# One expert's projection gathered into a block of twelve matmuls, and the first silu moved to the chunk before, in a time-mix and mixture-of-experts kernel

## The chip, the cores and the metric

The kernel runs on one core of one Trainium2 chip. The metric is the device time of one execution in microseconds (us); lower is better.

## The reference

The input is 4 batches of 1024 tokens with 128 features. Two time-mix layers (layer norm, three 128x128 projections k, v, r, a decaying scan over time, an output projection) are added to the input and layer-normed. A router then picks for each token the two best of 8 experts, each expert takes at most 307 tokens of a batch, and every expert computes this on its rows:

```
x = _layernorm(x + time_mix(x))
logits = x @ router_w + router_b            # top 2 of E = 8, softmax of the two
h = einp2 @ w_c_fc + b_c_fc                 # 128 -> 512
g = einp2 @ w_gate + b_gate                 # 128 -> 512
o = silu(h * g) @ w_c_proj + b_c_proj       # 512 -> 128
x = _layernorm(x + sum over the two experts of prob * o)
```

## The kernel before, in words

All work is written out by hand, engine by engine, in one order for each engine; semaphores tie them. After a head (batches 0 and 1 are mixed, batch 0 is routed) the program is four periods, one for each batch b. A period has 32 points: point = 4 e + j, for expert e (0 to 7) and chunk j (0 to 3) of the expert's 512 hidden features.

At each point TensorE first runs `hidden_pair` (L778 to L780): three matmuls for the gate and three for the up projection, with 308 columns, into one of two pairs of PSUM banks (pair0 at even points, pair1 at odd). ScalarE copies the gate out with its bias (`gate_copy`, L984), VectorE multiplies (`product`, L1299, prod_made). The pair of banks is free again when that product is made, so `hidden_pair` of a point waits for the product two points earlier:

```
                if c >= 2 or later(b):
                    pe.wait_ge(prod_made, nth(b, POINTS, c - 1))
```

ScalarE applies silu to two chunks at a time (`silu`, L991): chunks 0 and 1 of expert e at its point j = 2, chunks 2 and 3 at point j = 0 of the next expert. TensorE multiplies the result by the projection weights (`project`, L795, output ps_o) one expert behind, in twelve pieces (four chunks by three blocks of 104 rows; each piece shows as two records). VectorE copies ps_o out (`copy_out`, L1311), at j = 0 of the expert after the next. The last expert of a batch is projected whole at point 1 of the next period.

Between these, tables name what else each engine does at a point, before its next point. On TensorE: transposes for the mixing (`turn`, L619), the k, v, r matmuls (`kvr`, L639 to L651), `out` (L679), router logits (L695), counts (L709 to L724), transposes of expert rows (`turn_slots`, L756, at points 6, 18, 28, 29, 30). On ScalarE copies of the same (L912, L929, L939, L968). On VectorE `slots_low` (L1161), the mixing (`kv_of`, `scan_of`: L1112, L1122, L1127), statistics and norms (L1070, L1076, L1095), the combine of a finished batch (first_sum L1252, second_sum L1261, final_norm L1287). The mixing of batch b + 2 stands in period b, so only periods 0 and 1 have it; period 2 has the routing of batch 3, and period 3 has only the last combines. After period 3 comes a tail that adds the last batch's experts.

Of the kernel before, what the change touches and what calls it, by code (L numbers as in the profile page):

```python
# [37 lines left out]
B, T, L = 4, 1024, 2  # L38
# [5 lines left out]
E, K, H = 8, 2, 512  # L44
HC = H // P
# [3 lines left out]
PARTS = 3  # L49
# [110 lines left out]
               15: [("scales", 3)], 16: [("spread", 0)], 21: [("spread", 1)], 22: [("spread", 2)],  # L160
               23: [("spread", 3)], 24: [("spread", 4)], 29: [("spread", 5)]}

PIECES = ({j: tuple(range(4 * (j - 1), 4 * j)) for j in (1, 2, 3)}, {2: tuple(range(6)), 3: tuple(range(6, 12))})
PIECES_LAST = {1: tuple(range(6)), 2: tuple(range(6, 12))}
SLOT_TURNS = {6: (0, 3), 18: (0, 4), 28: (1, 0), 29: (1, 1), 30: (1, 2)}


# [7 lines left out]
def nth(b, per, k):  # L175

    return b * per + k


def step(b, n):  # L180


    return nth(b, 4, n + 1) if n < 4 else nth(b, 2, n - 3)
# [17 lines left out]
def later(b):  # L201

    return b > 0


def time_mix_moe(nc, h, ln_w, ln_b, Wk, Wv, Wr, Wo, router_w, router_b, w_fc, b_fc, w_gate, b_gate,
                 w_proj, b_proj, out):
    with ExitStack() as ctx:
# [379 lines left out]
        def _(pe):  # L588
# [142 lines left out]
            def turn_slots(b, g):  # L731
                mixed = min(step(b + 1, 3), 4 * B)
                if g == 0:
                    pe.wait_ge(r_copied, mixed)
                    pe.wait_ge(turned_sb[1], step(b, 5))
                if g == 1:
                    pe.wait_ge(k_copied, mixed)
                    pe.wait_ge(x_added, mixed - 1)
                    pe.wait_ge(rows_made, b + 1)
                if g == 2:  # L740
                    pe.wait_ge(kv_made, mixed)
                    pe.wait_ge(x_added, mixed)
                    pe.wait_ge(logits_copied, nth(b, 2, 2))
                if g < 2 and later(b):
                    pe.wait_ge(slots_copied, nth(b - 1, GROUPS, 4 + g))
                if g >= 3:
                    pe.wait_ge(slots_copied, nth(b, GROUPS, g - 2))
                if g == 3 and b + 1 < B:
                    pe.wait_ge(turned_sb[1], step(b + 1, 5))
                if g == 4 and b + 1 < B:  # L750
                    pe.wait_ge(rows_made, b + 2)
                if g == 4 and b + 2 < B:
                    pe.wait_ge(x_added, step(b + 2, 0))
                pe.wait_ge(slots_loaded[g], nth(b, 16, 16))
                for j in range(4):
                    mm = nc.tensor.transpose(bank[g % 3][:, P * j:P * j + P], slot_x[:, g % SLOT_RING, j, :],  # L756
                                             ident[:, :])
                mm.then_inc(slots_turned, 1)

            def hidden_pair(b, e, j):  # L760

                c = e * HC + j
                cols = slice(e * SLOTS, e * SLOTS + COLS)
                chunk = slice(P * j, P * j + P)
                if j == 0:
                    pe.wait_ge(slots_copied, nth(b, GROUPS, (e * SLOTS + COLS - 1) // (4 * P) + 1))
                if c == 0 and not later(b):
                    for read in (r_copied, k_copied, kv_made):
                        pe.wait_ge(read, nth(1, 4, 4))
                    pe.wait_ge(rows_made, 1)  # L770
                    pe.wait_ge(pool_low_made, 2 * LOW_BY_POOL)
                    pe.wait_ge(vector_low_made, 2 * (E - LOW_BY_POOL))
                    pe.wait_ge(x_added, step(1, 3))
                if c >= 2 or later(b):
                    pe.wait_ge(prod_made, nth(b, POINTS, c - 1))
                for which, (hi, lo, made) in enumerate(((gate_hi, gate_lo, g_made), (fc_hi, fc_lo, h_made))):
                    ps = pair[c % 2][which][:, 0:COLS]
                    nc.tensor.matmul(ps, hi[:, e, chunk], slotT_hi[:, cols], start=True, stop=False)  # L778
                    nc.tensor.matmul(ps, hi[:, e, chunk], slotT_lo[:, cols], start=False, stop=False)  # L779
                    nc.tensor.matmul(ps, lo[:, e, chunk], slotT_hi[:, cols], start=False, stop=True).then_inc(made, 1)  # L780

            def project(b, e, pieces):

                for piece in pieces:
                    c, part = divmod(piece, PARTS)
                    if piece == 0:
                        pe.wait_ge(hidden_made, nth(b, 2 * E, 2 * e + 1))
                        if e or later(b):
                            pe.wait_ge(o_copied, nth(b, E, e))
                        else:  # L790
                            pe.wait_ge(proj_in, 16 * E)
                            pe.wait_ge(x_added, step(1, 3))
                    if piece == 2 * PARTS:
                        pe.wait_ge(hidden_made, nth(b, 2 * E, 2 * e + 2))
                    mm = nc.tensor.matmul(ps_o[0:PART, P * part:P * part + P],  # L795
                                          hidden[:, e % 2, c, PART * part:PART * part + PART], proj_sb[:, e, c, :],
                                          start=(piece == 0), stop=(c == HC - 1), skip_group_check=True)
                    if piece == HC * PARTS - 1:
                        mm.then_inc(o_made, 1)
# [54 lines left out]
            def period(b):  # L854
                for point in range(POINTS):
                    e, j = divmod(point, HC)
                    hidden_pair(b, e, j)
                    if b == LAST:
                        for name, n in TENSOR_LAST.get(point, ()):
                            last_stages[name](n)  # L860
                    if b + 1 < B:
                        for name, n in TENSOR_ROUTE.get(point, ()):
                            stages[name](b + 1, n)
                    if e > 0:
                        project(b, e - 1, (PIECES[b + 2 < B] if nth(b, E, e) + 1 < B * E else PIECES_LAST).get(j, ()))
                    if point == 1 and b > 0:
                        project(b - 1, E - 1, range(HC * PARTS))
                    if point in SLOT_TURNS:
                        ahead, g = SLOT_TURNS[point]
                        if b + ahead < B:  # L870
                            turn_slots(b + ahead, g)
                    if b + 2 < B:
                        for name, n in TENSOR_MIX.get(point, ()):
                            stages[name](b + 2, n)
# [9 lines left out]
            for b in range(B):  # L884
                period(b)
# [10 lines left out]
        def _(act):  # L896
# [80 lines left out]
            def gate_copy(b, e, j):  # L977
                c = e * HC + j
                act.wait_ge(g_made, nth(b, POINTS, c + 1))
                if c == 0 and not later(b):  # L980
                    act.wait_ge(small_in, 16 * 2)
                if c >= 2 or later(b):
                    act.wait_ge(prod_made, nth(b, POINTS, c - 1))
                nc.scalar.activation(gate_s[:, c % 2, :], pair[c % 2][0][:, 0:COLS], ACT.Identity,  # L984
                                     bias=bgate_sb[:, e, j:j + 1]).then_inc(g_copied, 1)
# [19 lines left out]
            def period(b):  # L1005
                for point in range(POINTS):
                    e, j = divmod(point, HC)
                    gate_copy(b, e, j)
                    if b == LAST:
                        for name, n in SCALAR_LAST.get(point, ()):  # L1010
                            last_stages[name](n)
                    if j == 0 and e > 0:
                        silu(b, e - 1, 1)
                    if point == 0 and b > 0:
                        silu(b - 1, E - 1, 1)
                    if j == 2:
                        silu(b, e, 0)
                    if b + 1 < B:
                        for name, n in SCALAR_ROUTE.get(point, ()):
                            stages[name](b + 1, n)  # L1020
                    if point in SLOT_TURNS:
                        ahead, g = SLOT_TURNS[point]
                        if b + ahead < B:
                            copy_slots(b + ahead, g)
                    if b + 2 < B:
                        for name, n in SCALAR_MIX.get(point, ()):
                            stages[name](b + 2, n)
# [16 lines left out]
            for b in range(B):  # L1044
                period(b)
# [616 lines left out]
```

## Time and profile before

| what | value |
|---|---|
| median of 3 runs | 366.13 us (363.21 to 367.05) |
| profiled execution, first to last instruction | 382.6 us |
| TensorE busy in it | 332.7 us (87%) |
| VectorE, GpSimd, ScalarE busy | 262.8, 203.9, 166.2 us |
| periods 0, 1, 2, 3 in it | 69.94, 71.53, 68.19, 64.19 us |

The profile is of one execution, with its own time, longer than the median of the timed runs; the times give no other number for it. Its matmul ends are modelled. A matmul's record is longer than the time until the next one starts, so work on TensorE is best read from start to start. The same holds for VectorE, where records overlap by some 0.09 us.

### The profile page before, as it was taken

Reading aid. Unit: us, or ns where it says so; the run is one execution under the profiler, and the core shown is the slowest. Engines: PE = TensorE matmul, PEld = TensorE weight load, DVE = VectorE, ACT = ScalarE, POOL = GpSimd, SP = SyncE. Lnnn points to the kernel's source line nnn. Section 1 sums busy time; section 2 is a strip of 40 time slices with the busy share of each in tenths; the row PEclk is TensorE's granted clock in tenths of the full one; section 3 lists DMA queues with packets and bytes.
Section 4 is the critical chain, followed back from the end, with each engine's and each line's share of the span. In section 5 each row is a group of like instructions: output and inputs, shape, how many; then the busy total and the mean of one; then the engine's idle time right before and its main releaser. Section 6 shows DMA issues by size and latency. Waiting matters only on the chain.

```text
span 382.6 us, 7195 instructions
## 1 busy us (share of the span) xinstructions
PE 332.7 (87%) x2338; PEld 292.0 (76%) x2338; DVE 262.8 (69%) x853; ACT 166.2 (43%) x302; POOL 203.9 (53%) x244
## 2 busy tenths in 40 slices
PE   6889975869999999999999999877799986997880
PEld 3555653669879789997888999877689886987870
DVE  6688895787668868787787798831437684675225
ACT  2644434436545445555454445432435443363200
POOL 4185078850345642244557668377554437764752
PEclk9999896969999999999999999996999999898996
DMA  8949743150131133111114532222256111111152
GB/s 207 207 58 203 186 147 119 59 140 2 32 100 36 50 87 99 35 48 33 38 37 174 150 100 54 61 75 62 61 138 121 37 42 51 23 47 40 28 153 69
DMA packets 61246, 32.61 MB, mean 85 GB/s; under 512 B 15995, under 2 KB 58823, under 8 KB 61210
## 3 DMA queue, kind: packets, MB, share of 16 engines
q1 hardware_dynamic: 55322, 23.43, 25.3%
q0 software_dynamic: 4256, 7.94, 7.2%
q10 hardware_dynamic: 1632, 0.79, 0.7%
q8 instruction: 19, 0.31, 0.3%
q14 instruction: 17, 0.14, 0.1%
HBM read 19.01 MB, written 13.69 MB: 85 GB/s over the span
## 4 chain that ended last, share of the span: by engine, by line
PE 67%; issue 9%; DVE 8%; POOL 7%; another core or an unknown queue 3%; DMA 3%; ACT 3%; POOLq 0%; DVEq 0%; ACTq 0%
PE ps_o L795 20%; POOL slot_rows L1495 3%; PE pair0g L780 3%; PE pair0g L778 3%; PE pair1g L778 3%; PE bank L756 3%; PE bank L639 2%; PE pair1g L780 2%; PE bank L649 2%; PE pair0g L779 2%; PE bank L619 2%; PE pair1g L779 2%; PE bank L651 2%; PE pair1h L778 2%
## 5 line engine op out<-in xcount | busy, mean ns | idle before, releaser
L795 PE MATMUL ps_o<-proj_sb,hidden 128*104 128x128 f32 x768 | 99.7, 279 | 4.2 <-DVE o_sb L1311 2.1
L795 PEld LDWEIGHTS ps_o<-proj_sb,hidden 128*104 128x104 f32 x768 | 93.3, 175 | 5.8 <-issue 5.4
L1495 POOL DMA_INDIRECT slot_rows<-x_rows,row_to x64 | 72.5, 1133 | 45.1 <-DVE prod L1299 25.8
L1547 POOL DMA_INDIRECT picked<-expert_rows,row_from x48 | 49.9, 1039 | 37.4 <-DVE prod L1299 24.3
L984 ACT ACTIVATE gate_s<-pair0g,bgate_sb 128x308 f32<-128x308 f32 x64 | 33.1, 517 | 81.8 <-PE pair0g L780 52.7
L1299 DVE SCALAR_TENSOR_TENSOR prod<-pair1h,bfc_sb,gate_s 128x308 f32<-128x308 f32 x64 | 34.0, 532 | 32.3 <-ACT gate_s L984 17.7
L1299 DVE SCALAR_TENSOR_TENSOR prod<-pair0h,bfc_sb,gate_s 128x308 f32<-128x308 f32 x64 | 34.2, 534 | 26.4 <-ACT gate_s L984 11.8
L991 ACT ACTIVATE hidden<-prod 128x616 f32<-128x616 f32 x64 | 45.6, 712 | 7.7 <-DVE prod L1299 7.7
L984 ACT ACTIVATE gate_s<-pair1g,bgate_sb 128x308 f32<-128x308 f32 x64 | 33.0, 515 | 33.8 <-PE pair1g L780 22.2
L778 PE MATMUL pair1g<-slotT_hi,gate_hi 128*128 128x308 f32 x64 | 26.6, 416 | 10.0 <-DVE prod L1299 4.9
L1512 POOL DMA_INDIRECT returned<-o_sb,home x21 | 21.6, 1029 | 17.3 <-DVE prod L1299 11.2
L778 PE MATMUL pair0g<-slotT_hi,gate_hi 128*128 128x308 f32 x64 | 26.2, 409 | 4.0 <-DVE prod L1299 3.9
L1471 POOL TENSOR_TENSOR rstd<-shifted,power 128x4 f32<-128x4 f32 x24 | 26.2, 1093 | 2.0
L1311 DVE TENSOR_TENSOR o_sb<-ps_o,bproj_sb 104x384 f32<-104x384 f32 x32 | 17.5, 547 | 11.7 <-PE ps_o L795 7.4
L778 PEld LDWEIGHTS pair1g<-slotT_hi,gate_hi 128*128 128x128 f32 x64 | 12.4, 194 | 13.5 <-DVE prod L1299 6.7
L1467 POOL TENSOR_SCALAR shifted<-moments 128x4 f32<-128x4 f32 x24 | 6.8, 283 | 29.3 <-DVE moments L1076 29.1
L1161 DVE TENSOR_TENSOR slotT_lo<-bank,slotT_hi 128x512 fp32r<-128x512 f32 x20 | 13.8, 690 | 9.8 <-ACT slotT_hi L968 9.7
L1122 DVE TENSOR_TENSOR_SCAN kv_sb<-decay,kv_sb 128x512 f32<-128x512 f32 x16 | 20.1, 1255 | 0.6
L778 PE MATMUL pair0h<-slotT_hi,fc_hi 128*128 128x308 f32 x64 | 20.0, 312 | 0.0
L780 PE MATMUL pair0h<-slotT_hi,fc_lo 128*128 128x308 f32 x64 | 19.9, 312 | 0.0
L780 PE MATMUL pair0g<-slotT_hi,gate_lo 128*128 128x308 f32 x64 | 19.9, 311 | 0.0
L779 PE MATMUL pair0h<-slotT_lo,fc_hi 128*128 128x308 f32 x64 | 19.9, 311 | 0.0
(233 smaller groups left out, 773.0 us busy)
## 6 DMA issues: line engine op xcount, KB each, us to landing
slot_in<-slot_rows SPq DMA_DIRECT2D x20, 260.0 KB
expert_rows<-o_sb SPq DMA_DIRECT2D x24, 156.0 KB
x_in<-in_L_attn_h SPq DMA_DIRECT2D x4, 512.0 KB, 5.7
x_rows<-in_L_ffn_w_gate SPq DMA_DIRECT2D x8, 256.0 KB
x_rows<-in_L_ffn_w_c_fc SPq DMA_DIRECT2D x8, 256.0 KB
proj_sb<-in_L_ffn_w_c_proj SPq DMA_DIRECT2D x8, 256.0 KB, 5.3
out<-picked SPq DMA_DIRECT2D x12, 128.0 KB, 2.6
slot_rows<-slot_in SPq DMA_DIRECT2D x5, 260.0 KB, 7.2
```

The lines of the kernel that those rows point to most:

```text
L778: nc.tensor.matmul(ps, hi[:, e, chunk], slotT_hi[:, cols], start=True, stop=False)
L779: nc.tensor.matmul(ps, hi[:, e, chunk], slotT_lo[:, cols], start=False, stop=False)
L780: nc.tensor.matmul(ps, lo[:, e, chunk], slotT_hi[:, cols], start=False, stop=True).then_inc(made, 1)
L795: mm = nc.tensor.matmul(ps_o[0:PART, P * part:P * part + P], hidden[:, e % 2, c, PART * part:PART * part + PART], proj_sb[:, e, c, :], sta ...
L984: nc.scalar.activation(gate_s[:, c % 2, :], pair[c % 2][0][:, 0:COLS], ACT.Identity, bias=bgate_sb[:, e, j:j + 1]).then_inc(g_copied, 1)
L991: nc.scalar.activation(hidden[:, e % 2, 2 * i:2 * i + 2, 0:COLS], prod[:, e % 2, 2 * i:2 * i + 2, :], ACT.Silu).then_inc(hidden_made, 1)
L1122: nc.vector.tensor_tensor_scan(kv_sb[:, lo:hi], decay[:, :], kv_sb[:, lo:hi], kv_sb[:, lo - 1:lo] if n % 2 else 0.0, ALU.mult, ALU.add)\
L1299: nc.vector.scalar_tensor_tensor(prod[:, e % 2, j, :], pair[c % 2][1][:, 0:COLS], bfc_sb[:, e, j:j + 1], gate_s[:, c % 2, :], ALU.add, ALU ...
L1471: nc.gpsimd.tensor_tensor(rstd[:, r, norm, tiles], shifted[:, r, norm, tiles], power[:, 0:HT], ALU.pow)\
L1495: nc.gpsimd.indirect_dma_start(out=slot_rows, out_offset=bass.IndirectOffsetOnAxis(ap=row_to[:, c:c + 1], axis=0), in_=x_rows[:, b, c // K ...
L1512: nc.gpsimd.indirect_dma_start(out=returned, out_offset=bass.IndirectOffsetOnAxis(ap=home[:, PARTS * e + i:PARTS * e + i + 1], axis=0), in ...
L1547: nc.gpsimd.indirect_dma_start(out=picked[:, j, k, :], out_offset=None, in_=expert_rows[b % 2], in_offset=bass.IndirectOffsetOnAxis(ap=row ...
```

## The change

`PIECES` and `PIECES_LAST` split the projection of expert e - 1 over the points of expert e: in periods 0 and 1 six pieces at j = 2 and six at j = 3; in periods 2 and 3 four at each of j = 1, 2 and 3; for the very last expert six at j = 1 and six at j = 2. Now all twelve stand behind `hidden_pair` of j = 1. The silu of chunks 0 and 1 moves from behind the gate copy of j = 2 to behind that of j = 1. No instruction is added or removed.

```diff
-PIECES = ({j: tuple(range(4 * (j - 1), 4 * j)) for j in (1, 2, 3)}, {2: tuple(range(6)), 3: tuple(range(6, 12))})
-PIECES_LAST = {1: tuple(range(6)), 2: tuple(range(6, 12))}
+PROJECT_AT = 1
 SLOT_TURNS = {6: (0, 3), 18: (0, 4), 28: (1, 0), 29: (1, 1), 30: (1, 2)}
...
-                    if e > 0:
-                        project(b, e - 1, (PIECES[b + 2 < B] if nth(b, E, e) + 1 < B * E else PIECES_LAST).get(j, ()))
+                    if e > 0 and j == PROJECT_AT:
+                        project(b, e - 1, range(HC * PARTS))
                     if point == 1 and b > 0:
                         project(b - 1, E - 1, range(HC * PARTS))
...
-                    if j == 2:
+                    if j == PROJECT_AT:
                         silu(b, e, 0)
```

What it does to the order shows at points 14 to 18 of period 0 (experts 3 and 4). On TensorE, before; the first row ends `hidden_pair` of point 14, L679 is `out`:

```order
L780 MATMUL pair0h<-slotT_hi,fc_lo 128x308
L795 MATMUL ps_o<-proj_sb,hidden 104x128 x6
L679 MATMUL bank<-w_mix,mixed 128x128 x4
L778 MATMUL pair1g<-slotT_hi,gate_hi 128x308
...
L780 MATMUL pair1h<-slotT_hi,fc_lo 128x308
L795 MATMUL ps_o<-proj_sb,hidden 104x128 x6
L778 MATMUL pair0g<-slotT_hi,gate_hi 128x308
...
L780 MATMUL pair1h<-slotT_hi,fc_lo 128x308
L679 MATMUL bank<-w_mix,mixed 128x128 x4
L778 MATMUL pair0g<-slotT_hi,gate_hi 128x308
```

The same stretch now, from the end of point 13's pair on:

```order
L779 MATMUL pair1h<-slotT_hi,fc_lo 128x308
L794 MATMUL ps_o<-proj_sb,hidden 104x128 x12
L638 MATMUL bank<-normT,w_mix 128x512
...
L779 MATMUL pair0h<-slotT_hi,fc_lo 128x308
L678 MATMUL bank<-w_mix,mixed 128x128 x4
L777 MATMUL pair1g<-slotT_hi,gate_hi 128x308
...
L779 MATMUL pair1h<-slotT_hi,fc_lo 128x308
L777 MATMUL pair0g<-slotT_hi,gate_hi 128x308
...
L779 MATMUL pair1h<-slotT_hi,fc_lo 128x308
L794 MATMUL ps_o<-proj_sb,hidden 104x128 x12
```

The pairs of points 14, 15, 16 and 17 now have nothing between them but one `out`; the twelve pieces stand at points 13 and 17.

On ScalarE, the rows of points 14 to 17 before (gate copies of 14, 15, 16, 17; the first silu is of expert 3's first two chunks, the second of its last two):

```order
L984 ACTIVATE gate_s<-pair0g,bgate_sb 128x308
L991 ACTIVATE hidden<-prod 128x2x308
L984 ACTIVATE gate_s<-pair1g,bgate_sb 128x308
L984 ACTIVATE gate_s<-pair0g,bgate_sb 128x308
L991 ACTIVATE hidden<-prod 128x2x308
L984 ACTIVATE gate_s<-pair1g,bgate_sb 128x308
```

and now:

```order
L983 ACTIVATE gate_s<-pair0g,bgate_sb 128x308
L983 ACTIVATE gate_s<-pair1g,bgate_sb 128x308
L983 ACTIVATE gate_s<-pair0g,bgate_sb 128x308
L990 ACTIVATE hidden<-prod 128x2x308
L983 ACTIVATE gate_s<-pair1g,bgate_sb 128x308
L990 ACTIVATE hidden<-prod 128x2x308
```

The silu has left the place behind point 14's gate copy; that of expert 4's first two chunks stands behind point 17's.

## Rows read from the trace of the kernel before

**Rows 1.** The page's first part: busy us, share of the span, instructions.
```profile
PE 332.7 (87%) x2338; PEld 292.0 (76%) x2338; DVE 262.8 (69%) x853; ACT 166.2 (43%) x302; POOL 203.9 (53%) x244
```

**Rows 2.** Windows, one for each period: busy us (instructions), PEclk, DMA share, GB/s.
```profile
82.46:152.40 69.94, 69.13 (x502) 62.42 (x500) 53.37 (x164) 36.75 (x68) 26.12 (x29) 0.98 0.23 63
152.40:223.93 71.53, 70.62 (x527) 63.76 (x525) 56.16 (x178) 36.89 (x68) 37.24 (x40) 1.00 0.27 78
223.93:292.12 68.19, 59.63 (x462) 56.99 (x461) 38.78 (x131) 29.84 (x56) 43.28 (x50) 0.95 0.31 80
292.12:356.31 64.19, 55.76 (x410) 53.32 (x408) 40.78 (x117) 27.48 (x51) 37.99 (x43) 0.95 0.17 42
```

**Rows 3.** Timeline, points 22 and 23 of period 2: start, length, engine, [idle].
```profile
273.86 0.39 PE L778 MATMUL pair0g<-slotT_hi,gate_hi 128*128 128x308 f32 x1
274.57 0.52 ACT L984 ACTIVATE gate_s<-pair0g,bgate_sb 128x308 f32<-128x308 f32 x1 [1.21 <-PE pair0g L780]
275.19 0.54 DVE L1299 SCALAR_TENSOR_TENSOR prod<-pair0h,bfc_sb,gate_s 128x308 f32<-128x308 f32 x1 [1.19 <-PE pair0h L780]
275.59 0.39 PE L778 MATMUL pair1g<-slotT_hi,gate_hi 128*128 128x308 f32 x1
```

**Rows 4.** Timeline, VectorE, products 14 and 15 of period 0, mixing between them.
```profile
112.97 0.54 DVE L1299 SCALAR_TENSOR_TENSOR prod<-pair0h,bfc_sb,gate_s 128x308 f32<-128x308 f32 x1 [2.83 <-ACT gate_s L984]
...
116.14 0.53 DVE L1299 SCALAR_TENSOR_TENSOR prod<-pair1h,bfc_sb,gate_s 128x308 f32<-128x308 f32 x1
```

**Rows 5.** Timeline, points 6, 7 and 9 of period 0; last, one of period 1.
```profile
91.81 0.39 PE L778 MATMUL pair0g<-slotT_hi,gate_hi 128*128 128x308 f32 x1
94.41 0.39 PE L778 MATMUL pair1g<-slotT_hi,gate_hi 128*128 128x308 f32 x1
95.32 0.69 DVE L1161 TENSOR_TENSOR slotT_lo<-bank,slotT_hi 128x512 fp32r<-128x512 f32 x1 [0.89 <-ACT slotT_hi L968]
96.95 0.54 DVE L1299 SCALAR_TENSOR_TENSOR prod<-pair1h,bfc_sb,gate_s 128x308 f32<-128x308 f32 x1
98.16 0.39 PE L778 MATMUL pair1g<-slotT_hi,gate_hi 128*128 128x308 f32 x1
...
167.41 0.91 DVE L1319 MEMSET x_in<- 128x1024 f32 x1 [0.16 <-issue]
```

**Rows 6.** Timeline, VectorE, points 29 and 30 of period 1.
```profile
221.18 0.68 DVE L1161 TENSOR_TENSOR slotT_lo<-bank,slotT_hi 128x512 fp32r<-128x512 f32 x1
...
222.30 0.54 DVE L1299 SCALAR_TENSOR_TENSOR prod<-pair0h,bfc_sb,gate_s 128x308 f32<-128x308 f32 x1
```

**Rows 7.** Timeline, period 0: kvr of point 13, point 22, points 24 to 27.
```profile
109.01 1.10 PE L639 MATMUL bank<-normT,w_mix 128*128 128x512 f32 x2 [0.26 <-ACT normT L912]
...
129.54 0.39 PE L778 MATMUL pair0g<-slotT_hi,gate_hi 128*128 128x308 f32 x1
129.82 0.78 ACT L912 ACTIVATE normT<-bank,lnb_sb,lnw_sb 128x512 f32<-128x512 f32 x1 [0.34 <-PE bank L619]
...
139.26 0.53 DVE L1299 SCALAR_TENSOR_TENSOR prod<-pair0h,bfc_sb,gate_s 128x308 f32<-128x308 f32 x1
139.85 0.41 PE L778 MATMUL pair0g<-slotT_hi,gate_hi 128*128 128x308 f32 x1 [0.55 <-DVE prod L1299]
142.92 0.39 PE L778 MATMUL pair1g<-slotT_hi,gate_hi 128*128 128x308 f32 x1
```

**Rows 8.** Timeline, points 16 and 17 of period 2.
```profile
254.09 0.39 PE L778 MATMUL pair0g<-slotT_hi,gate_hi 128*128 128x308 f32 x1
257.22 0.41 PE L778 MATMUL pair1g<-slotT_hi,gate_hi 128*128 128x308 f32 x1 [2.02 <-issue]
260.98 0.52 ACT L984 ACTIVATE gate_s<-pair0g,bgate_sb 128x308 f32<-128x308 f32 x1 [5.28 <-remote]
```

**Rows 9.** A window in period 2, columns as in rows 2.
```profile
259.60:266.40 6.80, 6.08 (x26) 5.78 (x27) 1.58 (x3) 1.64 (x3) 5.30 (x7) 0.50 0.23 67
```

## The prediction

> **What bounds the kernel now.** I read the page's first part, then a window for each period, then the timeline of the points one by one. TensorE is busy 332.7 of 382.6 us [rows 1]. In periods 0 and 1 it is busy 69.13 of 69.94 and 70.62 of 71.53 us [rows 2]: no wait of any size is left there, so a change of order cannot gain much and every new wait adds to the end. In periods 2 and 3 it is idle for 8.56 and 8.43 us. Part of that belongs to the profiled execution alone. At point 16 of period 2 the pair starts at 254.09 and ScalarE's copy of it only at 260.98, where at point 22 the same copy follows after 0.71 us [rows 3, 8]; such late results of TensorE stand in periods 2 and 3 only. The median is 366.13 us, 16.5 below this span, so most of it is not in the timed runs. I make the sum as differences and add it to 366.1.
>
> The bare chain of one point is in [rows 3]: pair starts at 273.86, gate copy at 274.57, product from 275.19 to 275.73, so the product ends 1.87 us after its pair starts; and a pair that waits starts 0.06 us after the product (pair 26 of period 0, 139.79 to 139.85 [rows 7]). From pair to pair with eight records of the projection between, 1.73 us pass (273.86 to 275.59), of which 0.87 are the eight records (8 x 0.108): a pair takes 0.86, four pieces 0.87, twelve pieces 2.61 us. A pair waits for the product two points back, so it may start some 1.92 us after that pair did. Two bare pairs are only 1.72 us of work. The projection pieces between the pairs are what covers the difference now, and above all what covers VectorE's other work between two products.
>
> **What the change moves.** TensorE's work stays the same. After the block, the pairs of points 2, 3, 0' and 1' (0' and 1' are of the next expert) follow each other with only table work between them. Before, 2.61 us of projection lay between point 2 and point 0' (1.74 in periods 2 and 3, and 0.87 behind point 1). Take pair 2 as time 0. Pair 0' can start at 1.92 at the earliest, pair 1' at product 3's start + 0.54 + 0.05. The time by work alone is 1.72 and 2.58, plus table work. What pair 2' needs is covered by the block in either order.
>
> (a) No table work on either engine: 1.92 - 1.72 = 0.20 us for an expert. That holds in period 2 for experts 3, 5 and 6: 0.6.
>
> (b) Points 14 and 15, periods 0 and 1: VectorE makes the whole mixing between products 14 and 15, 3.17 us from start to start (112.97 to 116.14) [rows 4]. Product 15 starts at 1.33 + 3.17 = 4.50, and pair 17 at 5.09. By work it is 2.58 + 0.89 = 3.47; the 0.89 is `out`, from point 26, where a pair, twelve records and `out` take 3.07 (139.85 to 142.92 [rows 7]) and the first two 2.17. New wait 1.62 each, 3.24 in both. Today it is hidden by the 1.3 + 1.3 us of projection at 14 and 15.
>
> (c) Point 6, expert rows. A pair, twelve records and the four transposes take 2.60 (91.81 to 94.41 [rows 5]), so the transposes are 0.43 and end 1.29 after pair 2. ScalarE's copy and then VectorE's part follow, the latter 0.91 later (95.32): 2.20. Then 1.63 us until product 7 in period 0 (to 96.95), 2.52 in period 1, which blanks a buffer there (0.91 [rows 5], 0.89 from start to start). Pair 9 at 4.42 and 5.31, against 2.58 + 0.43 + 0.73 = 3.74 (0.73 are the counts of point 8: pairs 7 to 9 take 3.75, 94.41 to 98.16, with two pairs and twelve records in them): waits of 0.68 and 1.57. Period 3 has one sum of the combine instead, 1.12 us until the product [rows 6]: pair at 3.91 against 3.01, 0.90. Period 2 has longer counts: none.
>
> (d) Point 18, the same pattern: periods 2 and 3 0.90 each. In periods 0 and 1 a kvr (some 2.3) stands at point 20 and covers it.
>
> (e) Points 29 to 31 and 0, 1: transposes at 29 and 30, the first right behind the block. Product 30 at 0.91 + 1.12 = 2.03, product 31 at 2.03 + 0.45 + 1.11 = 3.59 [rows 6], pair 1' at 4.18 against 2.58 + 0.43 = 3.01: 1.17 in periods 1 and 2. Period 0 has no combine there: 0.38. Period 3 ends there: 0.
>
> (f) Single sums of the combine or scales at point 10 (period 2), 14 and 26 (period 3): product 3 at about 2.3 to 2.4: 0.31, 0.39, 0.31, together 1.0.
>
> (g) The kvr at points 10, 20 and 22 loses the projection between it and its transpose. The copy starts 0.28 after the transposes (129.54 to 129.82) and takes 0.78 [rows 7]; with 0.05 to the kvr that is 1.11, the pair between covers 0.86, 0.25 remains: six times, 1.5.
>
> Sum of new waits: 0.6 + 3.24 + 0.68 + 1.57 + 0.90 + 1.80 + 2 x 1.17 + 0.38 + 1.0 + 1.5 = 14.0 us.
>
> **What it takes away.** The block behind point 1 covers two waits of today in each of periods 0 and 1: kvr at 13 (0.26 shown as idle, 0.50 from the pair's end at 108.51 to 109.01), and the pair at 26 (0.55), both [rows 7]: 2.1 for both periods, and some 0.5 at points 9 and 11 of periods 1 and 2. Together 2.6. VectorE's copy out no longer waits for ps_o, but VectorE is no bound there: nothing.
>
> **The silu.** At j = 1 it waits for the product of the same point, and holds back the ScalarE queue: the gate copy of point 2 and the kvr copies. All of those need TensorE work behind the 2.61 us block, so pair 2's copy is due 3.47 + 0.71 = 4.18 after pair 1, and the silu is done at 1.87 + 0.75 = 2.6. Nothing, as long as product 1 ends within 3.4 us. It does not at point 17 of periods 0 and 1, where it ends near 4.9; the gate copy of 18 then comes 0.6 late, within the 0.7 which the table work at 18 leaves. If not, 1.2 more. Its leaving point 2 frees 0.3 us of ScalarE before gate copy 3, where VectorE is the later: nothing. No DMA moves except the stores of o_sb, whose copy out stands where it was.
>
> So 14.0 - 2.6 = +11.4, and **the forecast is 366.1 + 11.4 = 377.5 us**. A measurement of this kernel can tell about 1% (3.7 us) from no change.
>
> **Rivals.** (1) Half the waits: VectorE's queue is closer packed than my start-to-start readings, or waits overlap with one another. 7.0 - 2.6 = +4.4: 370.5. For it: in period 1 VectorE is busy 56.16 of 71.53 us [rows 2], so it has some room. Against: the mixing of (b) is a fixed 3.17.
>
> (2) Not slower: the late results of periods 2 and 3 [rows 8] are not only of the profile, and come of changing between projection and pairs at every point; the block, which changes once in four points, is free of them. Those periods hold 132.4 us of the span, so the timed runs leave them about 366.1 - (382.6 - 132.4) = 115.9, against some 106.3 of TensorE's own work (64 pairs, 16 projections, tables): at most 9.6 us to win. Its new waits in periods 0 and 1 (3.24 + 0.68 + 1.57 + 1.17 + 0.38 + 1.5 - 2.1 = 6.4) stay: 366.1 - 9.6 + 6.4 = 363. It decides if more than 6.4 of the 9.6 come back. Periods 0 and 1, which change too and show none, speak against it.
>
> The Trainium skill, "Perfetto Trace Analysis", section on the TensorE instruction's timeline, says that a matmul's end in the profile is computed and not observed. By that, what the late copy of [rows 8] waited for may be real work of TensorE; no row here shows which.
>
> (3) The clock. TensorE's granted clock is 1.00 (2.4 GHz) throughout period 1 [rows 2] and 0.50 (1.2 GHz) from 259.60 to 266.40, after an idle time of 2.02 and another like it [rows 8, 9]. My longest new wait is 1.62, and work follows on it. If it fell at experts 3 and 7 of periods 0 to 2, six times with 1.7 to 3.4 us lost (half of a stretch of 6.80, or of one half as long), the time would be 387 or more.
>
> The Trainium skill, "TensorE: Matmul & The Clock Gate", section on why this matters for kernels, warns that idle gaps between bursts of matmuls put the clock back to half. The trace agrees for the long idle of [rows 8]; by it this rival would hold if the waits add up.
>
> **How the numbers follow.** Forecast (373 to 383) 0.60; half the waits (369.8 to 373) 0.15; less than half (365 to 369.8) 0.11; rival 2 (359 to 365) 0.08, half of it faster by over 1%; clock 0.06. The range from 368 to 383 leaves out rival 2, the clock and part of the third case, 0.2 in all. Its upper end is the sum with 1.2 for the silu, 0.6 for a bare wait of twice the size, and 4 for readings from one execution. Slower by over 1%: 0.81; within 1%: 0.15; faster: 0.04.
>
> **What would show it.** Periods 0 and 1 longer by some 2 and 4 us; TensorE's L777 at pairs 17, 9 and 1 waiting for VectorE's product 1.2 to 1.6 us; the kvr (L638) at 10, 20 and 22 waiting 0.2 to 0.3 for normT; VectorE's copy out waiting for nothing. Wrong if pair 17 of period 0 starts within 4 us of pair 14, or if periods 2 and 3 get shorter in the timed runs.

## The result

The changed kernel takes 391.45 us (median of 4 runs, 391.32 to 393.54) against 365.35 us before (4 runs, 363.21 to 367.05): 1.074 times as long, 95% interval 1.068 to 1.080. It is 26 us slower, where 11.4 had been forecast.

The profiled execution of the changed kernel took 391.49 us, with 389.7 us from first to last instruction, so 1.8 us lie outside the span. By the same 1.8 us the timed runs of before have a span of some 363.5 us, and the 382.6 us of its profile were indeed an unusually long execution. The windows for the four periods, as in [rows 2]:

```profile
81.88:162.28 80.40, 72.00 (x501) 63.42 (x500) 52.65 (x162) 37.03 (x69) 26.66 (x29) 0.97 0.19 52
162.28:247.77 85.49, 75.74 (x525) 66.95 (x524) 57.03 (x177) 37.92 (x69) 37.00 (x39) 0.96 0.24 66
247.77:306.74 58.97, 56.66 (x460) 54.00 (x460) 38.73 (x132) 30.58 (x56) 42.58 (x48) 1.00 0.34 91
306.74:364.80 58.06, 53.91 (x406) 50.49 (x407) 39.66 (x117) 28.48 (x51) 38.50 (x43) 1.00 0.21 47
```

Period 0 grew from 69.94 to 80.40 us and period 1 from 71.53 to 85.49 us: 24.4 of the 26 us. Periods 2 and 3 are even shorter than in the long profiled execution of before, which says nothing. The timed runs of before leave 113 to 115 us for both (363.5 less the 250.2 outside them in the long execution, or with the head and tail of the changed kernel's trace in place of its own); here they take 117.0.

The waits of TensorE in the changed kernel, from the view of waits (us in total, how many, the longest; rows between are left out):

```profile
PE ps_o L794 <- DVE o_sb L1310: 13.0, 12, 2.5
PE pair1g L777 <- DVE prod L1298: 9.6, 11, 1.5
...
PE pair0g L777 <- DVE prod L1298: 0.9, 3, 0.3
```

The second and third rows are the waits that the prediction summed up. The first row is not in it at all. The projection waits for VectorE's copy out of the expert before. The timeline at point 13 of period 0 shows how:

```profile
107.43 0.54 DVE L1298 SCALAR_TENSOR_TENSOR prod<-pair1h,bfc_sb,gate_s 128x308 f32<-128x308 f32 x1 [3.01 <-ACT gate_s L983]
107.88 0.68 DVE L1111 TENSOR_TENSOR kv_sb<-bank,kv_sb 128x512 f32<-128x512 f32 x1
108.60 1.22 DVE L1121 TENSOR_TENSOR_SCAN kv_sb<-decay,kv_sb 128x512 f32<-128x512 f32 x1
109.93 0.69 DVE L1126 SCALAR_TENSOR_TENSOR mixed<-mixed,kv_sb 128x512 f32<-128x512 f32 x1
110.54 0.55 DVE L1310 TENSOR_TENSOR o_sb<-ps_o,bproj_sb 104x384 f32<-104x384 f32 x1
...
108.18 0.39 PE L777 MATMUL pair1g<-slotT_hi,gate_hi 128*128 128x308 f32 x1
...
111.24 2.84 PE L794 MATMUL ps_o<-proj_sb,hidden 128*104 128x128 f32 x24 [1.96 <-DVE o_sb L1310]
```

There is one ps_o. The block of expert 2 at point 13 may not start before expert 1 has been copied out. That copy stands on VectorE at j = 0 of expert 3, that is behind product 11 and the mixing of point 11. TensorE is done with pair 13 at 109.04, the copy ends at 111.09. Before the change, the same projection began at point 14, a pair and the kvr later, and nobody waited for the copy out in periods 0 and 1. In the changed kernel 11.9 of the 13.0 us are in these two.

The granted clock fell three times inside these two periods (a stretch that began in the head ends in period 0 before and now). In period 1 it had stayed at 1.00 before [rows 2]:

```profile
124.50:127.90 3.40, 3.40 (x19) 3.40 (x18) 1.56 (x5) 0.72 (x1) 2.48 (x3) 0.50 0.24 62
196.20:199.60 3.40, 3.40 (x18) 3.40 (x17) 0.37 (x3) 0.48 (x1) 2.88 (x4) 0.50 0.26 74
209.80:213.30 3.50, 3.50 (x18) 3.50 (x18) 1.68 (x6) 0.72 (x1) 2.79 (x3) 0.51 0.23 61
```

Each follows an idle time of TensorE in front of a block (point 17 of period 0, 13 and 17 of period 1). The block itself then takes 4.48 to 4.50 us in place of 2.84 above. Points 17 of period 0 and 13 of period 1:

```profile
121.56 0.41 PE L777 MATMUL pair1g<-slotT_hi,gate_hi 128*128 128x308 f32 x1 [1.45 <-DVE prod L1298]
...
124.01 4.50 PE L794 MATMUL ps_o<-proj_sb,hidden 128*104 128x128 f32 x24 [1.32 <-DVE o_sb L1310]
...
195.19 4.48 PE L794 MATMUL ps_o<-proj_sb,hidden 128*104 128x128 f32 x24 [2.48 <-DVE o_sb L1310]
```

So the theories for the runs were: (1) the block waits for the copy out, which stands behind VectorE's other work, and the clock falls in those waits; (2) the silu at j = 1 holds ScalarE's queue; (3) pairs wait for products, more than was reckoned.

### The profile page after: what moved, and what is told of

It is laid out like the page before. It is cut to its first block, busy times and chain, and to the rows that moved or that the text cites. A ratio compares the mean times of both kernels' runs of the same rounds, so it can differ in the third digit from the quotient of the medians.

```text
span 389.7 us, 7195 instructions
## 1 busy us (share of the span) xinstructions
PE 334.8 (86%) x2338; PEld 289.4 (74%) x2338; DVE 262.1 (67%) x853; ACT 169.4 (43%) x302; POOL 205.3 (53%) x244
## 4 chain that ended last, share of the span: by engine, by line
PE 52%; DVE 17%; POOL 12%; issue 11%; DMA 3%; ACT 3%; DVEq 0%; POOLq 0%; SPq 0%; ACTq 0%
PE ps_o L794 20%; DVE kv_sb L1121 3%; PE bank L638 3%; POOL picked L1546 2%; DVE prod L1298 2%; POOL returned L1511 2%; PE bank L648 2%; ACT gate_s L983 2%; PE bank L650 2%; POOL slot_rows L1494 2%; PE bank L755 2%; DVE o_sb L1310 2%; DMA picked<-expert_rows,row_from 2%; DVE kv_sb L1111 2%; PE pair0g L777 2%
## 5 line engine op out<-in xcount | busy, mean ns | idle before, releaser
L794 PE MATMUL ps_o<-proj_sb,hidden 128*104 128x128 f32 x768 | 95.5, 283 | 13.2 <-DVE o_sb L1310 13.0
L794 PEld LDWEIGHTS ps_o<-proj_sb,hidden 128*104 128x104 f32 x768 | 90.4, 178 | 17.4 <-issue 16.6
L1494 POOL DMA_INDIRECT slot_rows<-x_rows,row_to x64 | 73.3, 1145 | 52.5 <-DVE prod L1298 33.9
L777 PE MATMUL pair0g<-slotT_hi,gate_hi 128*128 128x308 f32 x64 | 24.2, 378 | 1.3 <-DVE prod L1298 0.9
L778 PE MATMUL pair0g<-slotT_lo,gate_hi 128*128 128x308 f32 x64 | 19.6, 306 | 0.0
```

The lines of the kernel that those rows point to most:

```text
L794: mm = nc.tensor.matmul(ps_o[0:PART, P * part:P * part + P], hidden[:, e % 2, c, PART * part:PART * part + PART], proj_sb[:, e, c, :], sta ...
L1494: nc.gpsimd.indirect_dma_start(out=slot_rows, out_offset=bass.IndirectOffsetOnAxis(ap=row_to[:, c:c + 1], axis=0), in_=x_rows[:, b, c // K ...
```

## The experiments

Every ratio is against the kernel before on the same chips (medians 364.3 to 365.1 us).

**The silu alone.** Before, with the silu of chunks 0 and 1 at j = 1:

```diff
-                    if j == 2:
+                    if j == 1:
                         silu(b, e, 0)
```

> Only the silu of the first two chunks moves to j = 1; the projection stays in pieces. Theory 1 (the block waits for the copy out of ps_o, which stands on VectorE behind the work of the point before): nothing of that here, so the time of before, 365 us, within 1%. Theory 2 (the silu at j = 1 holds ScalarE's queue, and the gate copies behind it come late): most of the 26 us, 380 us or more. Theory 3 (pairs wait for products because nothing stands between them): the time of before.

Measured 370.90 us, 1.017 (1.011 to 1.023). All three theories had missed this: the silu costs 6.3 us by itself. Periods 0 and 1 took 71.0 and 74.6 us (69.9 and 71.5 before), which is 4.1 of them. ScalarE at points 9 and 10 of period 0:

```profile
100.27 0.72 ACT L991 ACTIVATE hidden<-prod 128x616 f32<-128x616 f32 x1 [1.53 <-DVE prod L1299]
100.90 0.76 ACT L912 ACTIVATE normT<-bank,lnb_sb,lnw_sb 128x512 f32<-128x512 f32 x1
```

The silu waits for product 9, and the copy of the transposes (L912) for the silu. The transposes had been ready before: in the kernel before, that copy started at 99.73, in front of the silu. The kvr of point 10 then waits for the copy; from pair 10 to pair 11 it is 5.20 us in place of 4.43, and 5.74 in place of 4.42 in period 1. Point 1 of period 1 takes 0.79 us more. Where the other 2 us come from is not shown. In period 2 TensorE waits 2.2 us for a load at point 28, and a stretch of half clock follows (281.3); but the run with the change in periods 0 and 1 only shows the same wait and a fall behind it (303.9), with the silu of period 2 where it was.

**The block alone.** The changed kernel with the silu back at j = 2:

```diff
-                    if j == PROJECT_AT:
+                    if j == 2:
                         silu(b, e, 0)
```

> Only the projection becomes a block at j = 1; the silu stays at j = 2. Theory 1: the time of the changed kernel, 391 us, within 1%. Theory 2: near before, 366 to 370 us. Theory 3: 391 us too.

Measured 396.22 us, 1.085 (1.078 to 1.092): the block is what costs. It is 4.8 us above the changed kernel, outside the 1% expected. 1.7 of these are a fourth stretch of half clock (at 112.5, point 13 of period 0: 9.58 us from pair 13 to pair 14 against 7.91), 1.2 are at point 17 of period 1, where the stretch is longer. So 2.9 of the 4.8 us are clock, and the silu's move, 6.3 us of loss by itself, is no loss behind the block. TensorE's idle time in front of the block of point 13 is 1.96 us in both traces, and the clock fell behind it in one of them only.

**The block with an early copy out.** The changed kernel, and on VectorE:

```diff
-                    if j == 0 and e > 1:
-                        copy_out(b, e - 2)
-                    if point in (0, 2) and b > 0:
-                        copy_out(b - 1, E - 2 + point // 2)
-                    if b == LAST and point == POINTS - 1:
-                        copy_out(b, E - 2)
+                    if j == 2 and e > 0:
+                        copy_out(b, e - 1)
+                    if point == 2 and b > 0:
+                        copy_out(b - 1, E - 1)
```

> The changed kernel, with VectorE's copy out of an expert moved from j = 0 of the expert after the next to j = 2 of the next, just before that point's product, so that ps_o is free long before the next block. Theory 1: the 13.0 us that TensorE idles for o_sb go, and with them the three stretches of half clock in periods 0 and 1 (124.5, 196.2, 209.8), 1.7 us each: 391.5 - 13 - 5 = 373 us, 370 to 376. Theory 3: those waits only turn into waits of the pairs for products, since VectorE has the same work to do: 385 us or more.

Measured 370.74 us, 1.016 (1.011 to 1.022), within the range of theory 1. The silu and the block stand as in the changed kernel, so 20.7 us of its time hang on the place of the copy out. The waits of TensorE now:

```profile
PE pair1g L777 <- DVE prod L1298: 7.8, 10, 1.4
...
PE pair0g L777 <- DVE prod L1298: 3.6, 5, 0.9
```

No row names o_sb for ps_o, and VectorE waits for the projection instead, as the view of line L794 says:

```profile
who waited for it (us, times):
  DVE o_sb L1310: 19.5, 16
```

The periods take 73.22, 75.08, 59.18 and 54.76 us. Behind the stretch that ends at 86.0, early in period 0, there is no half clock up to 362.5, in the tail. Periods 0 and 1 are 17.6 us shorter than in the changed kernel, and period 3 is 3.3 us shorter, though TensorE waited for o_sb there only 0.7 us with the tail. In the changed kernel VectorE waits 1.8 us for gathered rows in period 3 (L1251), with a product queued behind; here it does not.

**Block and silu at j = 2,** copy out where it was:

```diff
-PROJECT_AT = 1
+PROJECT_AT = 2
```

> Block and silu both at j = 2 instead of j = 1, copy out where it was (j = 0). The copy out then has one point more before the block needs ps_o. Theory 1: most of the 13.0 us of waits for o_sb go, 368 to 376 us. Theory 3: pairs 3, 0', 1', 2' follow each other as barely as before, so about as slow as the changed kernel, 385 us or more.

Measured 379.40 us, 1.041 (1.036 to 1.047): between the two. The waits for o_sb are gone but for 0.61 us in period 1, and the clock holds. But pairs now wait for products, 3.97 us in period 0 and 4.29 in period 1, and the periods take 74.41 and 77.39 us. So 12 us of the loss of the changed kernel go with the room that the copy out has. The range of theory 1 was too low, and theory 3's part is only some of what it left out: against the early copy out, 3.5 us more stand in periods 0 and 1, and 4.9 in period 3 (59.22 against 54.76) and the tail.

**The copy out at j = 3:**

```diff
-                    if j == 2 and e > 0:
+                    if j == 3 and e > 0:
                         copy_out(b, e - 1)
```

> As e3_block_early_copy, with the copy out at j = 3 instead of j = 2, still ahead of the work that VectorE does between product 3 and product 0'. Theory 1 says that only the work standing ahead of the copy matters: the same as with j = 2, 369 to 373 us. If it is the distance to the block that counts instead, it should lie between 371 and 391, about 378.

Measured 378.27 us, 1.037 (1.033 to 1.041). The figure is that of the rival, its reason is not: TensorE waits for o_sb 0.55 us in all, against 13.0 in the changed kernel. The copy now stands in front of product 3, for which pair 1' waits, and that pair starts 0.47 us later at points 9, 17 and 1 (2.47 to 2.93 us from pair 16 to pair 17). In period 1 the clock falls once (at 197.7) and costs 1.66 at point 17; period 3 takes 57.45 us against 54.76. So a copy ahead of the other work is not enough; it must also stay out of the way of the product that is due next.

**The change in periods 0 and 1 only, and in 2 and 3 only.** Silu and block as changed where `b + 2 < B`, else as before, and the other way round:

```diff
-                    if e > 0 and j == PROJECT_AT:
-                        project(b, e - 1, range(HC * PARTS))
+                    if e > 0 and b + 2 < B:
+                        project(b, e - 1, range(HC * PARTS) if j == PROJECT_AT else ())
+                    elif e > 0:
+                        project(b, e - 1, (PIECES[b + 2 < B] if nth(b, E, e) + 1 < B * E else PIECES_LAST).get(j, ()))
...
-                    if j == PROJECT_AT:
+                    if j == (1 if b + 2 < B else 2):
                         silu(b, e, 0)
```

> The change in periods 0 and 1 only; 2 and 3 as before. Theory 1: the waits for o_sb (11.9 of 13.0 us) and all three stretches of half clock are there, where VectorE makes the mixing: +22 to +26, 387 to 391 us. Rival (the loss belongs to the bare pairs of periods 2 and 3, hidden in the traces compared so far because the profiled run of before was a long one): under 375 us.

> The change in periods 2 and 3 only. From the traces, these two take 117.0 us in the changed kernel; the timed runs leave before about 114.3: 365 + 3 = 368 us, 366 to 370. By the recorded prediction's own terms (5.5 of new waits there, 0.5 removed) it would be 370. Rival: over 375 us.

Measured 393.87 us, 1.077 (1.071 to 1.083), and 366.19 us, 1.005 (1.003 to 1.008). The second lies in its range. The first is 2.9 us above its own, and 2.4 above the changed kernel: its trace has a fourth stretch of half clock, at point 13 of period 0 (112.7; that point takes 9.58 us against 7.91) behind the same idle time of 1.96, and the wait of 2.2 us for a load at point 28 of period 2. All the loss but about 2 us belongs to the two periods in which VectorE makes the mixing.

**One step of the mixing moved.** The early copy out, and the mixing of half 1 behind product 15:

```diff
-... 11: [("mix", 0)], 14: [("mix", 1)], 15: [("add", 0), ("stats", 2)],
+... 11: [("mix", 0)], 15: [("mix", 1), ("add", 0), ("stats", 2)],
```

> e3_block_early_copy with one more step moved: VectorE's mixing of half 1 from behind product 14 to behind product 15. This tests term (b) of the prediction, a wait of pair 17 for product 15 of 1.62 us in each of periods 0 and 1 (1.45 shown in the changed kernel): 370.7 - 3.1 = 367.6 us, 366.5 to 368.7. If VectorE's work is the bound itself, the wait comes back at another pair: 370 to 371.

Measured 372.34 us, 1.021 (1.016 to 1.025), 1.6 above the early copy alone: above both ranges given, and in the direction of the rival. The wait of pair 17 went (from pair 16 to pair 17 0.98 us in place of 2.47), and came back behind it: 5.06 in place of 4.39 at point 17, 2.65 in place of 1.73 at 18, 1.87 in place of 0.94 at 19. Two of these are waits of pairs and transposes for later work of VectorE:

```profile
PE bank L618 <- DVE normed L1094: 6.1, 3, 4.7
PE pair0g L777 <- DVE prod L1298: 5.9, 9, 0.9
```

(In the view of the early copy alone these rows are 4.7 us in one wait and 3.6 us in five.)

**The norm of point 6 moved** to point 7, with the blanking in period 1, on top of the early copy out:

```diff
-VECTOR_MIX = {6: [("norm", 0)],
+VECTOR_MIX = {7: [("norm", 0)],
...
-                    if b + 2 == LAST and point == 6:
+                    if b + 2 == LAST and point == 7:
                         blank()
```

> e3_block_early_copy with VectorE's norm (and in period 1 the blanking of a buffer) moved from behind product 6 to behind product 7, where the block of point 9 covers it. Tests term (c): pair 9 no longer waits for product 7, 0.6 us in period 0 and 1.5 in period 1: 370.7 - 2.1 = 368.6, 367.8 to 369.5. If VectorE's work comes back at a later pair, as the mixing did when it was moved: 370.5 or more.

Measured 368.63 us, 1.010 (1.006 to 1.014), as expected. From pair 8 to pair 9 it is 1.50 us in both periods, in place of 2.20 and 3.10. Here the work moves behind the product that is due and under the block of point 9. It is not free everywhere: in period 1, point 10 takes 4.28 us in place of 3.41. Product 9 stands behind the blanking, the norm and other work on VectorE and ends 4.42 us after its pair starts (171.81 to 176.23). The silu waits for that product, the copy of the transposes (L911, at 176.89) stands behind the silu, and the kvr waits 0.93 us:

```profile
176.26 0.72 ACT L990 ACTIVATE hidden<-prod 128x616 f32<-128x616 f32 x1 [3.22 <-DVE prod L1298]
```

So 2.3 us were won at pair 9 and 0.87 came back; another 0.4 of the gain is at point 7 of period 2 (1.46 us in place of 1.87).

**The idle time filled.** The changed kernel with small matmuls, of whose result nothing is used:

```diff
+                    if b + 2 < B and point in (13, 17):
+                        pe.wait_ge(k_copied if point == 13 else r_copied, step(b + 2, 0 if point == 13 else 1))
+                        for _ in range(16):
+                            nc.tensor.matmul(bank[1 if point == 13 else 0][:, 0:P], ones[:, :], ones[:, :],
+                                             start=True, stop=True, skip_group_check=True)
                     if e > 0 and j == PROJECT_AT:
                         project(b, e - 1, range(HC * PARTS))
```

> The changed kernel with 16 small bf16 matmuls of ones, whose result nobody reads, in front of the blocks of points 13 and 17 of periods 0 and 1, where TensorE idles 1.3 to 2.5 us for ps_o. They add work only where it idles. If the idle time brings the half clock there (124.5, 196.2, 209.8 in the trace of the changed kernel, 24 records in 4.50 and 4.48 us instead of 2.84): those stretches go, 391.5 - 5 = 386.5 us, 385 to 388. If the clock falls for another reason: 391 to 393.

Measured 385.20 us, 1.055 (1.051 to 1.059). The three stretches of half clock are gone, and points 17 of period 0, 13 and 17 of period 1 are 1.67 us shorter each: 5.0 in all. Point 13 of period 1:

```profile
191.10 1.07 PE L866 MATMUL bank<-ones 128*128 128x128 bf16 x16
193.74 2.84 PE L794 MATMUL ps_o<-proj_sb,hidden 128*104 128x128 f32 x24 [1.57 <-DVE o_sb L1315]
```

TensorE still waits until VectorE's copy is done, but then the block runs in 2.84 us. The other 1.3 us between the medians cannot be placed: the two traces differ by +1.5 us in period 2 (with a wait of 1.33 for a load at point 28) and by -1.6 in period 3.

**The early copy out with the silu at j = 2:**

```diff
-                    if j == PROJECT_AT:
+                    if j == 2:
                         silu(b, e, 0)
```

> e3_block_early_copy with the silu back at j = 2: the silu's part of the change where no half clock blurs it. Recorded prediction (the silu at j = 1 is hidden by the block and costs or gains nothing): 370 to 371.5 us. If the gate copy of point 3 behind the silu delays product 3 and with it pair 1': 371.5 to 375.

Measured 372.91 us, 1.022 (1.017 to 1.026), which is in the range of the rival, the delayed product 3. From pair 8 to pair 9 it is 0.25 us longer in periods 0 and 1, which is product 3 behind a later gate copy, at point 31 of period 0 0.61 shorter. 1.61 us of the difference are one stretch of half clock (at 174.2, point 9 of period 1), behind a single idle time of 1.68 us; in the block-only trace 1.69 us at the same place brought none. Apart from the clock the silu's place behind a block is worth a few tenths of a microsecond.

**Pieces, then block.** Periods 0 and 1 as before, 2 and 3 with the block and silu as changed, and the copy out at j = 2 in period 3 alone (`if b == LAST and j == 2 and e > 0: copy_out(b, e - 1)`):

> Periods 0 and 1 as before the change (pieces at j = 2 and 3), periods 2 and 3 with the block, and the early copy out in period 3 alone. Spans by period from the traces: 69.9 and 71.5 (before), 58.1 (block in period 2 only), 54.8 (block and early copy in period 3), head and tail 82 and 24.5: 360.8 + 1.8 outside the span = 362.6 us, against 364.3 of before. If the period times do not add up so, 364 to 366.

Measured 362.54 us, 0.994 (0.991 to 0.996): faster than both kernels. The period times add up as expected: 69.72, 71.51, 58.07 and 55.02 us. The gain is the copy out's, not the block's: the change in periods 2 and 3 only differs from this kernel in nothing but the place of the copy out in period 3, and takes 366.19 us, 3.7 more than this kernel and 1.9 more than before. Whether pieces in all four periods, with as early a copy out as they allow, would be faster still was not tried.

## Why the prediction was wrong

**The direction and its place** were right: slower, by waits of TensorE that the split pieces had covered, mostly in the periods in which VectorE has the mixing.

**The step that failed** is the last sentence of the part on what the change takes away: "VectorE's copy out no longer waits for ps_o, but VectorE is no bound there: nothing." It looked at the semaphores between copy out and projection in one direction only. The block starts a point earlier, so it also needs ps_o free a point earlier, and the copy that frees it stays behind the work of the point before. That is a wait of 13.0 us in 12 places (some 0.2 more each from start to start, as 7.91 against 5.73 us at point 13 of period 0 for 1.96 of idle), 11.9 of it in periods 0 and 1. With the three stretches of half clock (5.0 us) it makes some 19 of the 24.4 us by which these two grew. The early copy out is 20.7 us faster by the medians and 20.4 shorter in the two traces. Of these 20.4, the 19 go, 1.5 come back at point 31 (1.99 and 1.90 us in place of 0.93 and 1.44), 3.3 are won in period 3 and 0.7 in the tail, and the head and period 2 are 1.2 longer. The 3.3 are for the most part not waits for o_sb; how much of them comes of gathered rows that arrive in time is not shown.

**The clock** was rival 3, at 0.06, for idle times at experts 3 and 7. Its mechanism came true at points 13 and 17, with 1.67 us for each stretch, the lower end of the 1.7 to 3.4 given, and three stretches in place of six. What brought it were idle times that the sum did not have. That idle time is the cause in these three places, the filled waits have shown. But the length of one wait does not decide it: an idle time of 1.96 us at point 13 of period 0 brought the half clock in two of the traces (block only, change in periods 0 and 1 only) and not in that of the changed kernel. The prediction's argument was that its longest wait, 1.62 us, is shorter than an idle of 2.02; yet at 124.5 the clock fell after idles of 1.45 and 1.32 us with a pair between them, and with the early copy out and the silu at j = 2 it fell after a single one of 1.68. The Trainium skill, "TensorE: Matmul & The Clock Gate", section "Why this matters for your kernels", warns of idle gaps between bursts of matmuls. The trace agrees that gaps bring the half clock, but those here are shorter than the gap that the page names.

**The waits that were summed** held for periods 0 and 1. Without the waits for o_sb (the early copy out) these periods are 73.22 + 75.08 - 69.94 - 71.53 = 6.8 us longer than before; the sum had 6.4. That the two are so near is in part luck, since 1.5 of the 6.8 are the waits at point 31 that the early copy out itself brings; without them it is 5.3. Term (b) had 1.62, and 1.45 of idle are shown; term (c) 0.68 and 1.57, shown 0.54 and 1.43, and moving the norm took back 2.1 us, though not all of it at pair 9. Term (b) was right as a wait, but not as something to be had back by moving its cause: VectorE's mixing only came out at the next pair.

**Periods 2 and 3** had 5.5 - 0.5 = 5.0 us in the sum; measured alone they cost 1.9 (366.19 against 364.25). These waits were too large, or before had more of its own there than the long profiled execution let me see. The traces of the silu alone and of the change in periods 0 and 1 only, which keep the pieces in period 2, show one such wait: 2.2 us for the load at point 28, where that of the change in periods 2 and 3 only has none. How often the timed runs of before have it, and so which of the two it was, stays open.

**The silu** was put at nothing, because the block covers it. Behind the block that is what the runs show, apart from the clock, as long as the prediction's own condition holds, that product 1 ends within 3.4 us of its pair: with the norm moved it ended after 4.42 in period 1, and 0.87 us were lost. It is the block's cover that makes it so. Alone the silu costs 6.3 us, 4.1 of them in periods 0 and 1, where the copies behind it on ScalarE come late.

**Rival 2,** late results of TensorE from changing between pairs and projection, is refuted: the change in periods 0 and 1 only keeps the pieces in periods 2 and 3, and there its gate copies start at most 1.41 us after their pairs, against 6.89 in the long profiled execution of before. The block in periods 2 and 3 alone made the time longer, not shorter. The 115.9 us that the rival gives the timed runs for these periods take a time for a span; without the 1.8 us outside it they are 113 to 115, so there was less to win. What delayed that execution was not tried.

## What to carry to other kernels

When a consumer of a single buffer is moved forward, look who frees the buffer and what stands ahead of that instruction on its own engine. A step that is hidden in both directions today (the copy waits for the projection, the projection for the copy) can turn round: here the copy mostly waited for the projection before, and now the projection waits for the copy.

Work that is split into pieces between dependent steps covers latency; gathered, it covers only what stands at one place. Whether that is a loss depends on the other engines' load: here 24 us in the periods with heavy VectorE work, 2 us in the others. The fastest version that was tried has the block in the light periods, but owes its gain to the copy out that was moved forward there.

Do not conclude from one idle time that did not lower the clock that shorter ones are safe: here the same idle time lowered it in one execution and not in another, and two of 1.45 and 1.32 us with a pair between them did. If waits cannot be removed, unused small matmuls in the idle time may win back more than they cost (5.0 us here, at three points).

## What the runs showed of the hardware

The granted clock fell to half after idle times of 1.3 to 2.5 us in front of a block, though TensorE was busy 72.00 of 80.40 and 75.74 of 85.49 us in those periods. Sixteen bf16 matmuls of 128 columns, 1.07 us together, in front of an idle time of 1.57 us kept it at full. Behind an idle time of 1.96 us at the same place of the program it fell in two traces and stayed in one.

Twelve pieces of fp32 projection take 2.84 us, first start to last end, at 2.4 GHz and 4.48 to 4.50 us where the clock is 1.2 GHz for most of them.
